# A memset after every gather: GpSimd clears a strip of unused memory between indirect DMAs

## What is computed

```python
h = relu(layernorm(x)); x = x + L0(h)   # attention over edges, 4 heads, batchnorm and a feed-forward part
h = relu(layernorm(x)); x = x + L1(h)   # two weighted sums: rows of support[src] to dst, and of support[dst] to src
h = relu(layernorm(x)); x = x + L2(h)   # two convolutions, each segment_sum(x[src]) and a product with x itself
h = relu(layernorm(x)); x = x + L3(h)   # attention over edges, 8 heads
```

## Time and profile before

| | |
|---|---|
| median of three runs | 10575.17 us (10565.06 to 10585.32) |
| the profiled execution | 10629.75 us, its span 10628.0 us |
| busy | TensorE 5936.1 us (56%), VectorE 4831.8 us (45%), ScalarE 2018.0 us (19%), GpSimd 5350.6 us (50%) |
| DMA | 1375.07 MB, mean 129 GB/s |

### The profile page before, as it was taken

How to read it: one execution, slowest core, us unless ns; L and a number is a source line. 1 busy time by engine, 2 the same in 40 slices (tenths; PEclk the granted TensorE clock), 3 DMA queues, 4 the chain that set the end, 5 groups by cost and what they waited for, 6 DMA issues and landing times. The chain is left out here.

```text
span 10628.0 us, 131026 instructions
## 1 busy us (share of the span) xinstructions
PE 5936.1 (56%) x24674; PEld 4756.4 (45%) x24675; DVE 4831.8 (45%) x13494; ACT 2018.0 (19%) x5480; POOL 5350.6 (50%) x5364
## 2 busy tenths in 40 slices
PE   4788886674656666645554454454455633222376
PEld 2687775553544444433333343333343432222254
DVE  6344446776544444435554233343333411112777
ACT  2111111783322222200000000010000300000276
POOL 3555552000068888876665666646666056664000
PEclk9777877997877777766666677777777655555699
DMA  4554556563067777754444333323333156665265
GB/s 148 163 158 157 166 160 208 181 200 106 2 113 105 104 105 105 104 120 142 142 142 130 91 89 91 89 82 87 91 90 90 60 165 196 188 195 151 77 200 181
DMA packets 848105, 1375.07 MB, mean 129 GB/s; under 512 B 112503, under 2 KB 501429, under 8 KB 847749
## 3 DMA queue, kind: packets, MB, share of 16 engines
q0 software_dynamic: 315328, 634.04, 27.1%
q1 hardware_dynamic: 398452, 575.30, 16.7%
q10 hardware_dynamic: 133968, 161.50, 4.8%
HBM read 949.47 MB, written 420.93 MB: 129 GB/s over the span
## 5 line engine op out<-in xcount | busy, mean ns | idle before, releaser
L1028 POOL DMA_INDIRECT regionB<-table,gather_rows x2352 | 2283.5, 971 | 1400.9 <-POOLq L1025 765.4
L1028 POOL DMA_INDIRECT regionC<-table,gather_rows x1568 | 1508.6, 962 | 861.2 <-issue 453.4
L1760 POOL DMA_INDIRECT scatter_sums<-regionC,idx x880 | 1383.7, 1572 | 306.2 <-issue 247.5
L1128 PE MATMUL ps_p<-regionB,hot 128*128 x3520 | 998.5, 443 | 846.4 <-DVE regionC L1189 511.6
L1128 PEld LDWEIGHTS ps_p<-regionB,hot 128*128 128x128 f32 x3520 | 782.9, 226 | 1035.6 <-issue 903.7
L1496 PE MATMUL ps_p<-regionA 128*128 128x266 f32 (+1 forms) x3520 | 848.4, 394 | 336.1 <-PEq L1491 216.2
L1128 PE MATMUL ps_p<-regionC,hot 128*128 x1760 | 621.7, 498 | 561.2 <-issue 487.5
L1965 PE MATMUL psS<-dst_scores,regionA 128*128 x1760 | 393.3, 362 | 897.3 <-PEq L1963 616.8
L1496 PEld LDWEIGHTS ps_p<-regionA 128*128 128x128 f32 x3520 | 653.2, 190 | 531.1 <-DVE regionC L974 194.2
L1965 PEld LDWEIGHTS psS<-dst_scores,regionA 128*128 128x128 f32 x1760 | 383.6, 330 | 907.1 <-issue 907.1
L1128 PEld LDWEIGHTS ps_p<-regionC,hot 128*128 128x128 f32 x1760 | 419.6, 249 | 763.3 <-issue 704.1
(11 more groups left out here) (309 smaller groups left out, 8503.1 us busy)
## 6 DMA issues: line engine op xcount, KB each, us to landing
regionA<-edge_rows SPq DMA_DIRECT2D x880, 256.0 KB, 3.3
edge_rows<-regionB SPq DMA_DIRECT2D x196, 512.0 KB
edge_rows<-regionC SPq DMA_DIRECT2D x392, 256.0 KB
regionC<-srcrow_d SPq DMA_DIRECT2D x220, 256.0 KB
scatter_sums<-zero_rows ACTq DMA_DIRECT2D x8, 6400.0 KB, 41.6
regionA<-scatter_sums ACTq DMA_DIRECT2D x49, 1024.0 KB
regionB<-table,gather_rows POOLq DMA_INDIRECT x2352
regionB<-rrow_d ACTq DMA_DIRECT2D x110, 256.0 KB
```

The source lines that it names most:

```text
L1028: g.indirect_dma_start(out=rows_of(b * per + j), out_offset=None, in_=table, in_offset=bass.IndirectOffsetOnAxis(ap=idx[:, column:column + ...
L1128: x = te.matmul(ps[(u.c * VG + j) % NB], hot[:, b, 2 * j + k, :], at_tile(G, slot[j] * 2 + k), start=k == 0, stop=k == 1)
L1760: g.indirect_dma_start(out=scat, out_offset=bass.IndirectOffsetOnAxis(ap=idx[:, b, j:j + 1], axis=0), in_=sums[:, b, j, :], in_offset=None ...
```

## The change

`gather` gets a memset after each indirect DMA. It clears 192 columns of all partitions behind the tiles of region B, which nothing reads or writes. A semaphore that is set to 1 ahead of the loop goes along: each memset first waits for the memset before it, which stands one gather earlier, and takes the 1 back. After the loop GpSimd waits for the last memset. All five passes use `gather`, so 3920 memsets are added.

```diff
         C = sb('regionC', [P, NT * 264])
+        breath = B[:, NT * D + 150:NT * D + 150 + 192]
...
+        s_breath = sem('s_breath')
...
                     for j in range(per):
                         column = at + half * per + j
                         g.indirect_dma_start(out=rows_of(b * per + j), ...).then_inc(s_rows[b].sem, 16)
+                        g.wait_ge(s_breath, 1)
+                        g.sem_inc(s_breath, -1)
+                        g.memset(breath, 0.0).then_inc(s_breath, 1)
+            g.sem_inc(s_breath, 1)
             for t_ in turns(g, steps, ring, 1):
...
                 if t_.has(1):
                     fetch(t_.at(1))
+            g.wait_ge(s_breath, 1)
+            g.sem_inc(s_breath, -1)
```

## The result

The changed kernel takes 10319.85 us (median of 4 runs, 10302.39 to 10332.62), the kernel before, run beside it, 10572.9 us (10565.06 to 10585.32). The ratio is 0.9758, with a 95% interval from 0.974 to 0.9777: faster by 253 us. The forecast was 10465, so the direction holds and the time lies in the range, but the gain was put at 112 us. In the ratios of this document one execution isn't used: one of the four of the 120-column kernel on chip D took 11667.2 us, 11% longer than the others.

The account below looks back on a forecast made before the run. GpSimd's gather issue sets the pace, interrupted by freezes of the other engines. Plain passes -9, layer 3's pass -103, layer 0's 0: -112 us on 10629.75, scaled to the plain runs' median: 10465 us, range 10275 to 10700.

Parts of the forecast that it names:

- layer 0's pass: Fetch of layer 0: 149 us of memsets fit into GpSimd's 431 us of slot waits under TensorE's work; change 0.
- The freeze and the pace: Gathers 1.253 us apart build a shared backlog that stalls other engines; at 1.443 us it should never build.
- Bounds of 1.36 and 1.41: Service time per gather, at most 1.41 us from l2a's ring and 1.36 us from layer 3's.
- The memset's price: Each memset between gathers adds 0.19 us, from spacing of starts; bounds 0.07 to 0.26, break-even 0.226 us.
- The rival with 0.13: Memset hides in the gap between gathers like the index copy, price 0.13 us: 10278 us; chance 0.14.
- The wait: Each memset's semaphore wait priced at nothing, covered by the gather's 0.95 us; uncovered about 0.3 us a gather.
- The plain passes: l1, l2a, l2b at 1138 us each: +6, -8 and -7, together -9 us; memsets replace stalls.
- the ring: GpSimd's wait for a free slot before a gather (line 1025 before): hardly any left in l2a.
- Layer 3's pass: Fetch of layer 3: 94 us to the 49th gather plus 1065 us for 736 more, 1159 against 1262: -103 us.
- rival 2: Memset costs more than it gains, perhaps held up by VectorE: 0.26 us each, 10679 us, slower; chance 0.13.

Follow-up runs that it names:

- 120-column kernel: Memset of 120 columns instead of 192 in the kernel after, a wait each: 9965.86 us, 1.0466 on B; 10476.04 us, 0.9894 on chip D.
- chip D: One of four further chips, used on one occasion; the unchanged kernel before takes 10578.9 us there.
- C: One of four further chips, used on one occasion; the unchanged kernel before takes 10684.25 us there, the kernel after 10497.36 us, 0.9822.
- E: One of four further chips, used on one occasion; the unchanged kernel before takes 10649.69 us there, the kernel after 10430.31 us, 0.9781.
- one column: Memset of 1 column instead of 192 in the kernel after, same waits: 9633.09 us, 1.0116 on B; 10747.89 us, 1.0047 on C.
- B: One of four further chips, used on one occasion; the unchanged kernel before takes 9522.45 us there.
- one wait in four: Kernel after with 120 columns, four strips, one wait for every four gathers: 9926.63 us, 1.0425 on B; 10423.74 us, 0.9857 on chip D.

## What the prediction had right, and the step that failed

The step that failed is layer 0's pass: put at 0, it gave 185 of the 304 us by which the profiled execution got shorter. The mechanism, freezes that a slower pace removes, held where the kernel before has freezes.

**The freeze and the pace: right wherever the kernel before freezes.** That is in the first measurement and on C, D and E. Freezes come with gathers 1.25 us apart, go in part at 1.33 and mostly or in part at 1.39, are gone from layer 3's pass at 1.47, and one column with all its waits leaves them (on C). Bounds of 1.36 and 1.41 taken from the rings of one trace were about right, but it isn't a sharp edge: on C the pace of 1.39 leaves 318 us of the gauge, in the first measurement 63. And it isn't a property of the program: on B the pace of 1.25 freezes nothing.

**The memset's price: 0.14 us, not 0.19.** Pace 1.393 less 1.254. I had used the spacing of two tiny memsets; what counts is the gap of 0.30 us behind a gather, which takes up 0.14 of the 0.28. The rival with 0.13 had this price right. Its time of 10278 is nevertheless 42 us under the measured one: it too had layer 0's pass and the wait at nothing, and it too took the profiled execution to be slower than the median by a half per cent. That was 54.6 us before and only 5.8 after, so of 304 us between the profiled executions 253 are left between the medians.

**The wait: priced at nothing, cost about 28 us in a plain pass.** On B one column costs 110.6 us with no change of pace, of which 28.3, 29.9 and 27.8 us in the plain passes, 11.6 in layer 3's, and the rest, some 13, would be in layer 0's. This is the price of wait and memset together. I had argued that the 0.95 us of a gather cover the semaphore's way. They do, as the pace of 1.251 shows; not covered are the gaps of up to 2.4 us behind the sequencer. That a longer lead would cover all of them is argued.

**The plain passes: near, by two errors.** At 0.14 us l2a would take 784 x 1.393 = 1092 us, with 98 copies of 0.13 us 1105. The trace has 1141, and the waits of GpSimd there make the difference (us in total, times, longest): 26.4 us behind the memset's wait (line 1032), 11.6 us of the index copy, and for line 1027, the ring, as good as nothing, as forecast, where the kernel before had:

```profile
POOL regionB L1028 <- POOLq L1025: 172.8, 110, 7.1
```

The kernel after:

```profile
POOL regionB L1030 <- POOLq L1032: 26.4, 85, 3.8
POOL gather_rows L1020 <- POOLq L1038: 11.6, 6, 2.1
...
POOL regionB L1030 <- POOLq L1027: 1.3, 8, 0.2
```

The memset was 39 us a pass cheaper than forecast and the wait as much dearer.

**Layer 3's pass: right, -95 for -103.** The 49th gather starts 89.8 us after the first (forecast 94), no idle time of 20 us is left, and a unit comes every 11.66 us, with eight gathers:

```profile
8702.85 3.58 PE L1973 MATMUL psS<-dst_scores,regionA 128*128 x16 [8.14 <-issue]
...
8714.51 3.58 PE L1973 MATMUL psS<-dst_scores,regionA 128*128 x16 [8.08 <-DVE regionA L1992]
```

The remaining 736 gathers took 1077 us instead of 1065, although each is 0.05 us cheaper. Some 31 us of that is in 66 memsets that last over 0.35 us, up to 0.82; the timeline of all engines shows one of them:

```profile
8713.28 0.75 DVE L1992 TENSOR_SCALAR regionA<-regionA,lane_no 128x1024 f32<-128x1024 bf16 x1
8713.45 0.78 POOL L1033 MEMSET regionB<- 128x192 f32 x1
```

The memset begins while VectorE makes the spread one-hot and ends 0.20 us after it. So it is with all 66: each begins inside a tensor_scalar of VectorE and ends 0.19 us after its end. The plain passes have it too, only shorter, as VectorE's tensor_scalars there have 128 columns and last 0.3 to 0.5 us. The 130 memsets over 0.35 us of the three passes all begin inside one, and the longest lasts 0.41 us; one of l2a:

```profile
5903.11 1.65 DVE L961 TENSOR_SCALAR hot<-iota,rel 128x128 f32<-128x128 f32 x8
5903.77 0.40 POOL L1033 MEMSET regionB<- 128x192 f32 x1
```

This is the hold-up of rival 2, small where the prediction placed it and larger in a pass in which I hadn't looked for it.
The Trainium skill (SBUF — State Buffer, Who interferes with whom) says just that: a VectorE tensor_scalar in a two-port mode holds the shared ports, and the GpSimd instruction that comes second waits until it is over. The trace agrees with it in all 66 memsets, though it doesn't name VectorE's mode. In l2a it shows either side as the second: of the memsets that begin inside a tensor_scalar, 40 are held, beside tensor_scalars of 0.28 us, and beside the other 95 it is the tensor_scalar that is longer (0.37 us at the median). The prediction had set the rule aside because of l2a's copies, but of those of the kernel before only nine begin inside a tensor_scalar, which is little to refute it with.

**Layer 0's pass: "0", measured -185 us. This is the step that failed.** I took TensorE's 1217 of 1443 us for a floor under which GpSimd's waits could be filled. It wasn't one: a good part was visits at half the clock, and where the freezes went, the falls of the clock went too (50 before, 21 after, 12 with one column on B). The clock of 0.78 stood in the very row that I read the earlier trace rows, and the timeline of before holds both durations of a visit; 440 visits at 2.15 us are 946 us, and without freezes the pass took 1061 us (one column, on B), so it had up to 380 us to give. The other chips show the same term: on C the pass went from 1462 to 1334 us, -128 us against -187 us for the whole change, and on D the memsets of layer 0's pass alone gave 171 us. That freezes and clock go together is shown; that the first cause the second is read from the timeline of one moment, and how the 185 us divide between them is the estimate above.

**The end: 19 us not forecast.** Behind layer 3's last gather the kernels with 1.39 us or more in that pass need 852 us, those with 1.33 on D 860 and 864, those with 1.25 on C, D and E and the kernel before 867 to 872, and on B all have 852. That fits rows that land late at the end of a frozen pass. It is argued, not shown.

**Left open.** What backs up, and why not on B. It isn't the bytes, and not the lead of GpSimd's queue. The pace was changed only by the length of a memset; gathers that are slowed by something else, and a memset without the wait, weren't tried.

## What to carry to other kernels

Before a busy engine is used as cover or as a floor, multiply its busy time by its clock: a TensorE at 84% busy and 0.78 of its clock has room (1217 x 0.78 = 949 us of work at full clock in a pass of 1443), and the shortest repetition of its pattern in the timeline tells how much. Where one engine issues small DMAs without a pause and all others stall at semaphores at once, a slower issue can be faster; choose the pace pass by pass. Work that needs no wait on the issuing engine might do it more cheaply; that wasn't tried. Measure such a change on several chips: the same edit gave -2.4% on one, -1.8% on another, and its 120-column form +4.7% on a third and -1.1% on a fourth.

## What the runs showed of the hardware

- The same kernel takes 9522 us on one chip and 10573 to 10684 in four measurements elsewhere, 11 to 12% apart. Whether that is the chip or its state on the one occasion that it was used, no run tells. GpSimd's gathers start 1.25 us apart on both kinds; in layer 3's pass the gauge goes from 38 us to 545 and more.
- A quarter of the gathered bytes changes the time by +0.3%, although in l2a the DMA engines are busy for 0.12 of the time instead of 0.31.
- A memset of 128x192 f32 is recorded with 0.28 us, costs 0.14 between two gathers and 0.42 in a chain of waits, and lasts up to 0.82 beside VectorE's tensor_scalar of 1024 columns.
- An index copy costs 0.13 us between a memset and a gather, and 0.07 between two gathers.
- A memset that begins inside a tensor_scalar of VectorE can be held until 0.19 us after its end: so with all 66 memsets over 0.35 us in layer 3's pass of the kernel after.
- The queue that the page calls instruction has 197 packets in the kernel before, 198 with the memset in layer 0's pass alone, 235 with one wait in four and 301 with one column and in the kernel after. GpSimd's gaps behind its sequencer in l2a are none with the memset in layer 0's pass alone, 10 with one wait in four, 16 with one column and 17 in the kernel after. Six of the 16 have such a packet and ten have none, so loading of code could explain the six at most.
